# Packing the late ranks of tiles 0 and 1 into one gathered list: 11 ring slots instead of 17, turns one chunk later

## What is computed

```python
# B = 512 users, K = 50 indices each (drawn up to about 99,999), V = 12,500 items, H = 512
retrieved = jnp.mean(item_embeddings[indices], axis=1)      # an index over V-1 reads the last item
fused_input = jnp.concatenate([user_rep, retrieved], axis=1)
fused_rep = fused_input @ W_fuse + b_fuse                   # [512,1024] @ [1024,512]
logits = fused_rep @ W_proj + b_proj                        # [512,512] @ [512,12500]
```

## Time and profile before

| what | us |
|---|---|
| median of 3 runs | 319.15 (318.23 to 319.33) |
| profiled execution, its own time | 319.95 |
| profiled execution, span | 317.9 |
| TensorE busy | 298.8 (94%) |
| VectorE busy | 248.4 (78%) |
| ScalarE busy | 129.1 (41%) |
| GpSimd busy | 83.8 (26%) |

### The profile page before, as it was taken

The page is one execution under the profiler, slowest core; times in us unless marked ns, Lnnn a source line. Parts: engine busy times, 40 slices in busy tenths (PEclk is TensorE's granted clock), DMA queues, the critical chain, the costliest instruction groups (busy, mean ns, idle before and its releaser), DMA issues.

```text
span 317.9 us, 4003 instructions
## 1 busy us (share of the span) xinstructions
PE 298.8 (94%) x1368; PEld 242.0 (76%) x1368; DVE 248.4 (78%) x354; ACT 129.1 (41%) x168; POOL 83.8 (26%) x84
## 2 busy tenths in 40 slices
PE   3968996989999999999999999999999999999995
PEld 1516874878879889888887888888888888888884
DVE  4899589894768883799869997979979798896123
ACT  1250436451002002325437665584556747563220
POOL 4778788876777710000000000000000000000000
PEclk9999996999999999999999999999999999999999
DMA  7995898989999621258728794948759296253315
GB/s 258 352 390 141 319 402 306 312 254 365 359 376 303 192 105 65 99 193 288 258 80 300 267 324 138 352 157 259 301 152 368 99 326 242 87 172 129 129 66 193
DMA packets 33348, 75.32 MB, mean 237 GB/s; under 512 B 5191, under 2 KB 21335, under 8 KB 33329
## 3 DMA queue, kind: packets, MB, share of 16 engines
q1 hardware_dynamic: 26416, 60.11, 52.9%
q0 software_dynamic: 6336, 13.92, 13.8%
q10 hardware_dynamic: 576, 1.05, 0.9%
HBM read 55.47 MB, written 25.60 MB: 255 GB/s over the span
## 4 chain that ended last, share of the span: by engine, by line
PE 67%; DVE 2%; issue 1%; ACT 0%; ACTq 0%
PE pair L1023 18%; PE pair L1082 15%; PE pair L1084 15%; PE pair L1085 15%; PE pair L1009 2%; DVE t_sums L811 0%; DVE early L813 0%; DVE w_lo L822 0%; PE pair L999 0%; ACT odd_sum L571 0%; DVE total L699 0%; DVE part_out L965 0%; DVE out_sb L766 0%; ACT w_hi L561 0%; ACTq L554 0%
## 5 line engine op out<-in xcount | busy, mean ns | idle before, releaser
L414 POOL DMA_INDIRECT ring<-item_embeddings,rows x68 | 71.7, 1054 | 23.8 <-issue 16.2
L1023 PE MATMUL pair<-w_hi,f_hi 128*128 128x500 f32 x144 | 57.3, 398 | 0.2
L1023 PE MATMUL pair<-w_lo,f_hi 128*128 128x500 f32 x144 | 57.2, 397 | 0.0
L1023 PE MATMUL pair<-w_hi,f_lo 128*128 128x500 f32 x144 | 57.0, 396 | 0.0
L1082 PE MATMUL pair<-w_hi,s_hi 128*128 128x500 f32 x128 | 49.8, 389 | 0.6 <-ACT odd_sum L571 0.6
L1084 PE MATMUL pair<-w_lo,s_hi 128*128 128x500 f32 x128 | 49.9, 390 | 0.0
L1085 PE MATMUL pair<-w_hi,s_lo 128*128 128x500 f32 x128 | 49.8, 389 | 0.0
L699 DVE SCALAR_TENSOR_TENSOR pair<-ring,mask,pair 128x512 f32<-128x512 f32 x56 | 42.1, 751 | 7.3 <-DMA ring<-item_embeddings,rows 4.1
L1084 PE MATMUL pair<-w_lo,f_hi 128*128 128x500 f32 x96 | 37.4, 390 | 0.0
L1082 PE MATMUL pair<-w_hi,f_hi 128*128 128x500 f32 x96 | 37.3, 389 | 0.0
L1085 PE MATMUL pair<-w_hi,f_lo 128*128 128x500 f32 x96 | 37.3, 388 | 0.0
(11 more groups left out here) (109 smaller groups left out, 416.8 us busy)
## 6 DMA issues: line engine op xcount, KB each, us to landing
w_raw<-w_proj SPq DMA_DIRECT2D x30, 500.0 KB, 7.7
logits<-part_out SPq DMA_DIRECT2D x21, 500.0 KB, 3.2
early<-w_proj SPq DMA_DIRECT2D x20, 500.0 KB, 5.6
logits<-out_sb SPq DMA_DIRECT2D x36, 250.0 KB, 3.7
logits<-out_sb SPq DMA_DIRECT2D x10, 500.0 KB, 3.0
early<-b_proj SPq DMA_DIRECT2D x8, 250.0 KB, 9.1
s_sum<-b_proj SPq DMA_DIRECT2D x8, 250.0 KB, 6.7
odd_bias<-b_proj SPq DMA_DIRECT2D x8, 250.0 KB, 5.9
```

The source lines that it names most:

```text
L414: return nc.gpsimd.indirect_dma_start(out=to, out_offset=None, in_=table, in_offset=bass.IndirectOffsetOnAxis(ap=column, axis=0), **how)
L1023: m = nc.tensor.matmul(ps[:, 0:CHUNK], f[:, t, k, :], w, start=begin, stop=(f is f_lo and k == HK - 1))
```

## The change

Tiles 0 and 1 use 11 slots (ranks 1 to 11), rank 12 is the lap, and the ranks from 13 up of all users are packed into one list of up to 128 row numbers, which is gathered once. To pack, VectorE counts each user's extra ranks; TensorE gives each user its offset (a product with a triangle `later`) and the total; VectorE compares places 1 to 128 with each extra's spot (`list_spots`, an array of 7 x 128 per user, held in the buffer of `wf_ret`); seven matmuls of 2 columns gather row number and user number per place (`pack_list`); VectorE writes the row numbers for the gather (`list_rows`) and a 0/1 matrix of place and user (`list_taken`), with which TensorE adds the gathered rows to the right users (`sum_in`). A list over 128 places or 7 extras falls back to laps. Tile 0's slots 0 to 5 are added on VectorE and 6 to 10 and the list on TensorE.

Moved besides: sorts of tiles 2 and 3 go into the stretch of tile 0's and of tile 1's chunks; turns from the middle of chunk 6 into the middle of chunk 7, and the fuse behind chunk 7; all of tile 1's adds ahead of tile 0's loop on VectorE; `wf_ret` is loaded once both lists are packed; chunks 2 to 7 go to four buffers in turn; ScalarE evacuates before it casts the next chunk, and issues the stores of tile 0 itself; the pace waits of the fourth user part are gone.

```diff
-PASSING = 17
+SLOTS = (11, 11, 17, 17)
+LISTING = 2
+LISTED = 7
-HOME_AT = 8
-LAPS_AT = 13
-DVE_FIRST = 11
+HOME_AT = (4, 4, 8, 8)
+LAPS_AT = (8, 8, 13, 13)
+DVE_FIRST = 6
-HOME_AFTER = 12
+HOME_AFTER = (0, 5, 12, 12)
...
         def raw_of(c):
-            return c if c < 4 else c % 2
+            return c % 4
...
             load_chunk(1)
+            sp.wait_ge(packed, LISTING)
             sp.dma_start(wf_ret[:], wf_dram[1]).then_inc(wf_ret_landed, 16)
             sp.wait_ge(user_fused, 1)
-            sp.wait_ge(slot_landed[place(0, PASSING - 1)], 16 * slot_uses(0, PASSING - 1))
-            for c in range(2, 6):
+            sp.wait_ge(slot_landed[place(0, SLOTS[0] - 1)], 16 * slot_uses(0, SLOTS[0] - 1))
+            for c in range(2, RESIDENT):
                 load_chunk(c)
...
+                    if i == SLOTS[t]:
+                        pool.wait_ge(listed, t + 1)
                     place_free(t, i)
...
-                    gather(ring[:, place(t, i), :], rows[:, t, i + 1:i + 2], **skip)\
-                        .then_inc(slot_landed[place(t, i)], 16)
+                    gather(ring[:, place(t, i), :], list_row[:, t:t + 1] if i == SLOTS[t] else rows[:, t, i + 1:i + 2],
+                           **skip).then_inc(slot_landed[place(t, i)], 16)
...
+            def list_spots(t):
+                then(nc.vector.scalar_tensor_tensor(spot[:, t, :], places[:, 0:LISTED], offset[:, t:t + 1],
+                                                    mask[:, t, static(t) + 1:static(t) + 1 + LISTED], ALU.add, ALU.mult))
+                nc.vector.tensor_tensor(spots[:, t, :, :], places.unsqueeze(1).to_broadcast([P, LISTED, P]),
+                                        spot[:, t, :].unsqueeze(2).to_broadcast([P, LISTED, P]), ALU.is_equal)\
+                  .then_inc(spots_ready, 1)
...
+            def pack_list(t):
+                pe.wait_ge(spots_ready, t + 1)
+                for j in range(LISTED):
+                    m = nc.tensor.matmul(list_ps[:, 2 * t:2 * t + 2], spots[:, t, j, :], listing[:, t, j, :],
+                                         start=(j == 0), stop=(j == LISTED - 1), skip_group_check=True)
+                m.then_inc(packed, 1)
             user_part(0)
-            user_part(1)
...
+            user_part(1)
+            pack_list(0)
             user_part(2)
+            pack_list(1)
             user_part(3).then_inc(user_fused, 1)
...
-                    halfway = t + 1 if c == RESIDENT - 2 and t + 1 < TILES else None
+                    halfway = t + 1 if c == RESIDENT - 1 and t + 1 < TILES else None
```

More of the change, by code:

```diff
@@ L124, in retrieval_scores @@
         bias_pick = f_hi[:, TILES - 1, 0, 0:RESIDENT]
-        kept = ([ret_t[:, k, :] for k in range(HK)] + [out_sb[:, 2, j * P:(j + 1) * P] for j in range(3)]
-                + [out_sb[:, 1, CHUNK - P:CHUNK]])
+        kept = [ret_t[:, k, :] for k in range(HK)] + [out_sb[:, 2, j * P:(j + 1) * P] for j in range(2)]
+        places = out_sb[:, 2, 2 * P:3 * P]
+        scratch = wf_ret[:, :, :].rearrange("p k n -> p (k n)")
+        spots = scratch[:, 0:LISTING * LISTED * P].rearrange("p (t j m) -> p t j m", t=LISTING, j=LISTED)
+        later = scratch[:, (LISTING * LISTED) * P:(LISTING * LISTED + 1) * P]
+        places_i = scratch[:, (LISTING * LISTED + 1) * P:(LISTING * LISTED + 2) * P].bitcast(I32)
+        token = listing[:, 0, 0, 1:2]
         fused_ps = banks[0:HK]
@@ L667, in count_columns @@
             def count_columns():
+                first, rest = most[:, 0:LISTING], most[:, LISTING:TILES]
+                base = static(TILES - 1) + 1
                 dve.wait_ge(counts_moved, 1)
                 then(nc.vector.tensor_reduce(most[:], first_ps[:, :].rearrange("a (t p) -> a t p", p=P), AX_X, ALU.max))
[L670 to L671 removed]
@@ L672, in count_columns @@
-                then(nc.vector.scalar_tensor_tensor(most[:], over[:, 0, :], float(BASE), over[:, 1, :],
-                                                    ALU.add, ALU.add))
-                nc.vector.tensor_scalar(laps_i[:], most[0:1, :], float(PASSING), None, ALU.subtract).then_inc(laps_ready, 1)
+                nc.vector.tensor_scalar(over[:, 0, LISTING:TILES], rest, base + 0.5, float(SORTED - base),
+                                        ALU.is_gt, ALU.mult)
+                then(nc.vector.tensor_scalar(over[:, 0, 0:LISTING], first, static(0) + 1 + LISTED + 0.5, None, ALU.is_gt))
@@ new lines, in count_columns @@
+                then(nc.vector.scalar_tensor_tensor(rest, over[:, 0, LISTING:TILES], float(base),
+                                                    over[:, 1, LISTING:TILES], ALU.add, ALU.add))
+                nc.vector.tensor_scalar(laps_i[:, 0:LISTING], most[0:1, 0:LISTING], float(SLOTS[0]), None, ALU.subtract)\
+                  .then_inc(laps_ready, 1)
+                nc.vector.tensor_scalar(laps_i[:, LISTING:TILES], most[0:1, LISTING:TILES], float(SLOTS[-1]), None,
+                                        ALU.subtract).then_inc(laps_ready, 1)
```

250 lines of the change are left out of this document (161 added, 89 removed).

## The result

| | kernel before | changed kernel |
|---|---|---|
| median of 6 runs each, us | 318.84 (318.23 to 319.33) | 322.66 (320.23 to 324.73) |
| ratio, 95% interval | | 1.0124 (1.0091 to 1.0156) |
| profiled execution, its own time | 319.95 | 320.23 |
| profiled execution, span | 317.9 | 318.4 |

The change costs 3.8 us. 316.6 was forecast, with a range of 314.0 to 320.3: both the sign and the range were wrong.

A forecast was written before the change was run, and what follows sets the result against it. Loads bound the head and VectorE then tile 0's chunks: head -0.2 us, tile 1's start -2.4, tile 2's -2.6 in all, so span 317.9 became 315.3 and the median 316.6 us, range 314.0 to 320.3.

The forecast's parts named there:

- a profiled kind of run: Whole kernel: span forecast 315.3 became 317.35 us for a profiled execution; the median of runs was put at 316.6.
- tile 1's stretch: Tile 1's first product to tile 2's: tile 1 forecast to begin at 73.5, tile 2 at 99.9 against 102.52.
- Slot 10 lands at about 25.8, with 3 us of latency: Head, gathers: tile 0's last slot gather, issued at 22.8, lands at about 25.8; SyncE's chunk loads then start 5.9 us earlier.
- F: Head: time of VectorE's first f_lo, set by the loads; forecast 38.2 against 37.96 before, ends 36.0 and 40.
- Rival 3: Head: f_hi behind the late chunk half; F = 43, 321.0 us, slower; no change reached at F = 41.2; chance 0.10.
- pack 1: Head, TensorE: second list's packing products, forecast to end at 21.3, when wf_ret is issued; rival 3 had it three us late.
- Rival 2: Tile 0's chunks: half clock at chunks 6 and 7 costs 3.6 us more, giving 320.2; chance 0.12.
- Rival 4: Tile 1: nothing gained, tile 2's lap at 90.8, 1.7 us later; tile 2 begins at 101.9, 318.5 us; chance 0.13.
- The packing: Head: list products 1.6 us each on TensorE, a spots array 1.06 us on VectorE, turn ending at 31.2 to 31.9.
- The gain of tile 0's chunks: Tile 0's chunks: waits and slow clock of 7.0 us go, VectorE binds; tile 1 begins at F + 35.3 = 73.5, -2.4 us.
- the middle: Start of tile 2: 99.9, taken between 100.2 held by tile 2's lap and 99.5 unheld; -2.6 us in all.

The follow-up runs named there:

- the first trace: Profiled execution of the changed kernel as first measured: own time 320.23 us, span 318.4; median of its six runs 322.66.
- the second trace: Profiled execution of the changed kernel timed once more without any edit: span 321.0 us; median 322.83 us, ratio 1.0096.
- four edits: Changed kernel without slot 10 wait before chunk loads, ScalarE's old head order, tile 2's sort with two tile 1 adds early, tile 2's home and lap early: 315.86 us.
- the early turn: Changed kernel with four edits, tile 1's turn back at chunk 6 of tile 0: ratios 0.9773, 0.981, 0.9701; with the three edits 0.9819.
- the three edits: Changed kernel without slot 10 wait before chunk loads, ScalarE's old head order, tile 2's sort and tile 1's first two adds early: 316.07 us, ratio 0.9918.

## Why the prediction was wrong

**Sum.** 317.35 was forecast for a profiled kind of run and 320.23 came: 2.9 us. The median was put 0.75 below that and lay 2.4 above it: 3.2 us more. Together they are the 6.1 us between 316.6 and 322.66. By the starts of tiles 1 and 2, the first trace lies 1.4 us over the forecast ahead of tile 1 (74.90 for 73.5) and 2.0 us more in tile 1's stretch (28.4 for 26.4).

**The step that failed: "Slot 10 lands at about 25.8, with 3 us of latency".** It measured 6.1 us in the first trace and longer in others, chunk 2 going out at 28.46 to 31.62 in the four traces of the changed kernel and its variants that left SyncE's waits and ScalarE's order alone. I chose between the 2.1 us of an idle queue and the median of 7.2 nearer the idle end. The 2.1 us belonged to the last slot before, a gather of almost no rows while the DMA engines stood idle. The change makes slot 10 the last, with rows of 75 users, 7.3 us earlier in a busy stretch (0.88), and puts wf_ret (22.66) beside it. With wf_ret held back it measured 3.6 us. With that wait taken out the trace lands on the forecast: F 38.48 for 38.2, tile 1 73.33 for 73.5, span 315.9 for 315.3. Its median is 318.72, not 316.6: its profiled execution too was the fastest of its runs. The time from the issue of chunk 2 to the cast of chunk 3's half, put at 11.0 us, was 10.3 and, with the early issue, 11.8.

**TensorE's wait before the fuse was not in the sum.** I saw that the mean stands behind a cast of chunk 2 now, and shifted f_hi, but asked of the mean only what the turn's end asks. 3.3 us without work before the fuse, and up to 6.5, are the result, and in four of five traces with such a wait the fuse ran at half clock: 6.2 to 6.7 us instead of 3.8. It did not move the end: in all five F is the start of the cast of chunk 3's first half plus 1.32 or 1.33 us. The median lies 2.4 us over the first trace because slot 10 mostly lands later than there: with it chunk 2, F, tile 1 and the span moved by 2.2, 2.3, 2.3 and 2.6 us in the second trace. That was a part of the same step, since the forecast took the difference between trace and median over from the kernel before.

**Rivals.** Rival 3 is what happened in mechanism and sign: F by the loads behind ScalarE's cast, with break-even put at F = 41.2. It had 0.10. (With tile 2 at F + 63.2, as measured, break-even is at F = 39.4.) Its F of 43 is within the 42.0 to 43.8 of four traces. Its cause (pack 1 late) is not: wf_ret went out at 22.66, 1.4 us after the forecast. Rival 2 put the half clock at chunks 6 and 7. TensorE waits 1.4 and 1.5 us there (2.1 and 1.7 forecast), and the clock stayed; it fell at the fuse instead. The Trainium skill's rule ("TensorE: Matmul & The Clock Gate", "HAM oscillation — how this bites in real kernels") speaks of waits for data longer than those at chunks 6 and 7, so the prediction read it too widely; it fits the fuse in four of the five traces. Rival 4's lap at 90.8 came at 90.80, but by luck: F was 1.9 us later than it had assumed.

**Right.** The packing: products of a list 1.62 and 1.72 us (1.6), array of spots 1.09 (1.06), tile 0's sum ends at 32.4 (31.2 to 31.9). The gain of tile 0's chunks: no wait and no slow clock at chunk 4, VectorE without gaps from F; tile 1 at F + 34.8 (F + 35.3). After tile 2 nothing changed: 215.1 us to the end, before 215.4.

**Tile 1's stretch** was put at 26.4 and took 28.4 us: waits of 0.9 and 1.1 us for evacuations, behind the lap at 90.80 and a store that VectorE waits 1.15 us for, and some 0.4 us more that I can't place. I had taken "the middle" between held and unheld. It varies between executions (27.4 to 28.6 us in the traces that leave the lap alone). Taking the lap away left it at 28.3 us with four edits, where a store is late next, and at 27.7 with that edit alone; the early turn isn't shown to shorten it either.

**Left open**: what the list gives by itself on a quiet chip; why slot 10 took 8.1 to 8.5 us in four executions and 6.1 in one; and whether wf_ret could be loaded early into another buffer (its own now holds the spots).

## What to carry to other kernels

A latency read from a nearly empty gather in an idle queue is void once the change makes another gather the last one and puts transfers beside it: price its landing by gathers of its size at its own time of the execution, and look for an engine in whose in-order queue something urgent (here the mean for TensorE) stands behind a step that waits for a load. And where VectorE's work from an event on sets the end, moving its work ahead of that event is worth most of its length (2.9 of 3.8 us here, and less once the loads come due: see the three edits), while a step that waits on the slowest transfer needs a bound by the range of several traces, not by one.

## What was not expected of the hardware

The clock's fall is not decided by the wait alone: after waits of 3.09, 3.81, 4.35 and 6.55 us the fuse ran mostly at 1.2 GHz, after one of 3.26 us wholly at 2.4 GHz. One gather's landing took 6.1 us in one execution and 8.1 to 8.3 in three others with the same order of transfers up to it. In one trace a megabyte in flight ahead of a 0.5 MB load made it take 10.2 instead of 5.9 us. And the same kernel before took 318.4 us on one chip, 335 to 340 us on two others; in the trace of the four edits there VectorE's waits show stalls that no engine or transfer ends:

```profile
DVE f_lo L839 <- issue: 7.6, 3, 5.3
...
DVE out_sb L856 <- remote: 7.0, 2, 5.7
```

What causes them was not found.
